# Relation attention, edge stage of a two-layer graph network: the mask goes into PSUM by matmuls, one maximum for all heads, the one-hot is transposed on TensorE

## The reference

```python
key_e = k_rel[edge_type, edge_src]
val_e = v_rel[edge_type, edge_src]
att = (q[edge_dst] * key_e).sum(-1) * rel_pri[edge_type] / jnp.sqrt(jnp.float32(dk))
seg = edge_dst * r + edge_type
amax = jax.ops.segment_max(att, seg, num_segments=S)
ex = jnp.exp(att - amax[seg])
denom = jax.ops.segment_sum(ex, seg, num_segments=S)
w = ex / denom[seg]
hsum = jax.ops.segment_sum(w[:, :, None] * val_e, seg, num_segments=S)
```

## Time and profile before

| what | us |
|---|---|
| median of three runs | 4749.34 |
| the three runs | 4734.86, 4749.34, 4750.56 |
| profiled execution, its span | 4737.6 |
| busy: PE, DVE, POOL, ACT | 4031.9, 4120.2, 3352.1, 2900.4 |
| HBM | 200 GB/s over the span |

### The profile page before, as it was taken

The page is one execution under the profiler, slowest core; times in us unless marked ns, Lnnn a source line. Parts: engine busy times, 40 slices in busy tenths (PEclk is TensorE's granted clock), DMA queues, the critical chain, the costliest instruction groups (busy, mean ns, idle before and its releaser), DMA issues. The chain is left out here.

```text
span 4737.6 us, 112614 instructions
## 1 busy us (share of the span) xinstructions
PE 4031.9 (85%) x23408; PEld 3334.4 (70%) x23408; DVE 4120.2 (87%) x13250; ACT 2900.4 (61%) x8405; POOL 3352.1 (71%) x3818
## 2 busy tenths in 40 slices
PE   0778888888888878999799898999999898968887
PEld 0357777777777767899677777777777677757776
DVE  6779999999999995555599999999999999968887
ACT  0765555555555543333488888888888888862222
POOL 0568888888888861111488888888888888857776
PEclk9989999999999998999888888888888888879899
DMA  2568777777777775666577777777777777776664
GB/s 75 179 206 250 229 228 228 228 228 227 228 229 228 228 190 174 202 200 197 168 207 206 204 206 204 206 204 205 205 204 206 204 204 204 205 158 189 176 170 133
DMA packets 647755, 950.12 MB, mean 201 GB/s; under 512 B 215768, under 2 KB 490760, under 8 KB 647287
## 3 DMA queue, kind: packets, MB, share of 16 engines
q0 software_dynamic: 153600, 510.70, 38.4%
q1 hardware_dynamic: 494043, 438.22, 32.1%
HBM read 777.56 MB, written 171.03 MB: 200 GB/s over the span
## 5 line engine op out<-in xcount | busy, mean ns | idle before, releaser
L1385 POOL DMA_INDIRECT kv1c<-kv_table,rec x936 | 916.8, 980 | 305.5 <-issue 175.2
L741 POOL DMA_INDIRECT kv<-kv_table,rec x864 | 921.3, 1066 | 247.3 <-issue 241.8
L1439 ACT ACTIVATE wv<-kv1c,wv 128x64 f32<-128x64 f32 x3744 | 927.7, 334 | 2.1
L1517 DVE CUSTOM_DVE_ANT_0 masked_scores<-score_p,mask 126x384 f32<-126x384 f32 x1248 | 679.5, 545 | 11.4 <-issue 5.8
L1615 PE MATMUL sum_p<-wv,hot 128*126 128x260 f32 x1872 | 626.3, 482 | 2.3 <-ACT wv L1439 2.3
L908 PE MATMUL sum_p<-msg,hot 128*126 128x256 f32 x1728 | 433.6, 394 | 192.2 <-DVE msg L864 192.2
L1577 PE MATMUL qe_p<-qrel,hotT 126*128 126x256 f32 x1872 | 546.9, 436 | 21.0 <-ACT hotT L1417 14.2
L1374 POOL TENSOR_SCALAR hot<-iota,local 128x126 f32<-128x126 f32 x936 | 549.7, 600 | 0.3 <-issue 0.2
L908 PEld LDWEIGHTS sum_p<-msg,hot 128*126 128x126 f32 x1728 | 309.4, 189 | 280.5 <-DVE msg L864 213.2
L1577 PEld LDWEIGHTS qe_p<-qrel,hotT 126*128 126x128 f32 x1872 | 428.8, 229 | 108.2 <-ACT hotT L1417 14.4
L1615 PEld LDWEIGHTS sum_p<-wv,hot 128*126 128x126 f32 x1872 | 398.4, 228 | 89.8 <-ACT wv L1439 2.7
(11 more groups left out here) (222 smaller groups left out, 10254.0 us busy)
## 6 DMA issues: line engine op xcount, KB each, us to landing
key<-segment_keys SPq DMA_DIRECT2D x312, 189.0 KB
q_blk<-q_table SPq DMA_DIRECT2D x216, 192.5 KB
acc_table<-acc SPq DMA_DIRECT2D x312, 128.0 KB
qrel<-q_by_relation SPq DMA_DIRECT2D x312, 126.0 KB
acc_in<-acc_table SPq DMA_DIRECT2D x50, 767.8 KB
q_by_relation<-qrel SPq DMA_DIRECT2D x50, 756.0 KB
feat<-in_edge_feat_t SPq DMA_DIRECT2D x216, 128.0 KB
agg_table<-total SPq DMA_DIRECT2D x216, 126.0 KB
```

What stands on the lines that cost most here:

```text
L741: pool.indirect_dma_start(kv[k][:, t, :], None, c["kv0_d"], bass.IndirectOffsetOnAxis(ap=rec[k][:, t, 0:1].bitcast(I32), axis=0)).then_inc ...
L1385: pool.indirect_dma_start(kv[k][:, t, :], None, c["kv1_d"], bass.IndirectOffsetOnAxis(ap=rec[k][:, t, 0:1].bitcast(I32), axis=0)).then_inc ...
L1439: ins = act.activation(wv[k][:, t, h, 0:DK], kv[s][:, t, D + h * DK:D + (h + 1) * DK], ACT.Copy, scale=wv[k][:, t, h, DK:DK + 1])
L1517: dve.tensor_tensor_reduce(junk[k][:, h, :], score_p[:, h, :], mask[it.slot(4)][:], 1.0, -BIG, ALU.add, ALU.max, top[s][:, h:h + 1]).then_ ...
```

## The change

In `edges_1`:

- The one-hot `hot` (edges by segments) is made by DVE in one instruction over all three tiles, at lag 0 (before: three on POOL at lag 1, behind `locate` on DVE). `locate` and the load of `key` go.
- ACT makes `cold` = 1 - hot in bf16 (lag 0); PE transposes it in three tiles (`turn_cold`, lag 1), and ACT makes the transposed one-hot in bf16 as 1 - cold, read from PSUM. `distances` and `masks` go.
- The mask gets into the scores' PSUM by three matmuls of 512 columns, cold times -2^100 on the diagonal, ahead of the twelve of `spread`, which now accumulate onto it.
- One `tensor_reduce` over 126x1536 takes the maxima of all four heads.
- `cap` goes; the split of the scores into bf16 parts moves from DVE to POOL (four small operations, between the gathers).
- The one-hot is bf16, so the queries come as three bf16 parts (nine matmuls of 256 columns in place of three f32) and the peak is split into three bf16 parts by four small operations on DVE (nine matmuls of 4 columns).
- ACT's scalings of values are split into three runs with other functions between.

In `nodes_1` the three bf16 parts of the queries are made: three copies on ACT, three subtractions on DVE, one more copy on ACT (126x1536) and one subtraction on POOL (126x1536). Each group's store grows from 756 to 1134 KB, each chunk's load of `qrel` from 126 to 189 KB.

The core of the diff:

```diff
@@ nodes_1
-                    for pair in range(1, PAIRS):
-                        ins = act.copy(qrel[k][:, 2 * pair:2 * pair + 2, :], rel_p[pair][:])
+                    for pair in range(PAIRS):
+                        act.copy(qrel[k][:, 2 * pair:2 * pair + 2, 0, :], rel_p[pair][:]).then_inc(rel_first, 1)
+                def rel_second_part(it):
+                    act.copy(qrel[k][:, :, 1, :], qrel_rest[k][:]).then_inc(rel_second, 1)
+                def rel_last_part(it):
+                    pool.tensor_tensor(qrel[k][:, :, 2, :], qrel_rest[k][:], qrel[k][:, :, 1, :],
+                                       ALU.subtract).then_inc(rel_last, 1)
+                def rel_left_over(it):
+                    for pair in range(PAIRS):
+                        dve.wait_ge(rel_first, it.count(0, PAIRS, pair + 1 - PAIRS))
+                        rels = slice(2 * pair, 2 * pair + 2)
+                        ins = dve.tensor_tensor(qrel_rest[k][:, rels, :], rel_p[pair][:], qrel[k][:, rels, 0, :],
+                                                ALU.subtract)
@@ relate (PE)
-                    wait(pe, rel_act, it, 1)
-                    wait(pe, rel_dve, it, 1)
+                    wait(pe, rel_left, it, 1)
@@ edges_1, POOL
-                run_chunks(pool, steps, ((5, fade_acc), (1, one_hot), (0, gather)))
+                run_chunks(pool, steps, ((0, gather((0,))), (2, lead_part(0)), (2, rest_part(0)), (2, lead_part(1)),
+                                         (2, rest_part(1)), (0, gather((1,))), (5, fade_acc), (0, gather((2,)))))
@@ ACT
+                def colds(it):
+                    wait(act, hot_ready, it)
+                    wait(act, spread_ready, it, 4)
+                    act.activation(cold[it.slot(4)][:], hot[it.slot(U)][:], ACT.Identity, bias=c["one"][:],
+                                   scale=-1.0).then_inc(cold_ready, 1)
                 def transposed_hot(it):
-                    wait(act, dist_ready, it)
+                    wait(act, coldT_turned, it)
-                run_chunks(act, steps, ((1, transposed_hot), (2, masks), (0, distances), (4, weights), (2, partsT_out)))
+                run_chunks(act, steps, ((4, weights), (0, colds), (4, values(0)), (1, transposed_hot), (4, values(1)),
+                                        (2, partsT_out), (4, values(2))))
@@ DVE
+                def one_hot(it):
+                    dve.scalar_tensor_tensor(
+                        hot[s][:], c["iota"][:].rearrange("p (o n) -> p o n", o=1).to_broadcast([P, T1, SEG]),
+                        par[s][:, 0:1], rec[s][:, :, 2:3].to_broadcast([P, T1, SEG]),
+                        ALU.add, ALU.is_equal).then_inc(hot_ready, 1)
-                        dve.tensor_tensor_reduce(junk[k][:, h, :], score_p[:, h, :], mask[it.slot(4)][:], 1.0, -BIG,
-                                                 ALU.add, ALU.max, top[s][:, h:h + 1]).then_inc(top_ready, 1)
+                    dve.tensor_reduce(top[s][:], score_p[:].rearrange("s t h e -> s h t e"),
+                                      mybir.AxisListType.XY, ALU.max).then_inc(top_ready, 1)
-                run_chunks(dve, steps, ((2, q_times_k), (4, below_peak), (2, scores), (4, cap), (0, locate),
-                                        (3, maxima(0)), (2, lead_part(0)), (3, maxima(1)), (2, rest_part(0)),
-                                        (3, maxima(2)), (2, lead_part(1)), (3, maxima(3)), (2, rest_part(1)),
-                                        (3, old_peak), (5, add_acc), (3, new_peak), (3, peak_drop)))
+                run_chunks(dve, steps, ((2, q_times_k), (4, below_peak), (2, scores), (3, old_peak), (0, one_hot),
+                                        (3, maxima), (5, add_acc), (3, new_peak), (3, peak_drop), (3, peak_part(0)),
+                                        (3, peak_part(1)), (3, peak_part(2)), (3, peak_part(3))))
@@ PE
+                def turn_cold(it):
+                    wait(pe, cold_ready, it)
+                    wait(pe, hotT_ready, it, 1)
+                    for t in range(T1):
+                        ins = pe.transpose(coldT_p[:, t * P:(t + 1) * P], cold[it.slot(4)][:, t, :], identity[:])
+                    ins.then_inc(coldT_turned, 1)
                 def q_of_edges(it):
-                        ins = pe.matmul(qe_p[:, t, :], hotT[k][:, t * P:(t + 1) * P], qrel[s][:], start=True, stop=True)
+                        for j in range(PARTS):
+                            ins = pe.matmul(qe_p[:, t, :], hotT[k][:, t * P:(t + 1) * P],
+                                            qrel[s][:, j * D:(j + 1) * D], start=j == 0, stop=j == PARTS - 1)
                 def spread(it):
+                    wait(pe, cold_ready, it)
+                    wait(pe, top_ready, it, 1)
+                    for t in range(T1):
+                        pe.matmul(score_p[:, t], cold[it.slot(4)][:, t, :],
+                                  mask_diag[:].rearrange("p (o e) -> p o e", o=1).to_broadcast([P, HEADS, P]),
+                                  start=True, stop=False)
                 def peaks_of_edges(it):
-                    wait(pe, peak_ready, it)
+                    wait(pe, peak_split, it, per=4)
+                            ins = pe.matmul(peak_p[:, t, :], hotT[k][:, t * P:(t + 1) * P],
+                                            peak_parts[it.slot(2)][:, j, :], start=j == 0, stop=j == PARTS - 1)
-                run_chunks(pe, steps, ((5, sum_values), (1, q_of_edges), (2, turn_parts), (3, peaks_of_edges),
-                                       (2, spread)))
+                run_chunks(pe, steps, ((5, sum_values), (1, turn_cold), (1, q_of_edges), (2, turn_parts),
+                                       (3, peaks_of_edges), (2, spread)))
```

`lead_part` and `rest_part`, written as before but for the engine, are on POOL now:

```diff
+                def lead_part(j):
+                        if j == 0:
+                            hold(pool, held, score_ready, it.count())
+                            wait(pool, partsT_turned, it, 2)
+                            pool.sem_inc(held, 1)
+                        else:
+                            hold(pool, held, split_ready, it.count(1, 4, 2 * j))
+                        pool.tensor_copy(parts[k][:, :, j, :], src[:]).then_inc(split_ready, 1)
```

More of the change, by code:

```diff
@@ L954, in nodes_1 @@
         qT_rest = [sb(f"qT_rest{k}", [P, HALF, GROUP], F32R) for k in range(2)]
-        qrel = [sb(f"qrel{k}", [GROUP, RELS, D]) for k in range(2)]
+        qrel = [sb(f"qrel{k}", [GROUP, RELS, PARTS, D], BF16) for k in range(2)]
+        qrel_rest = [sb(f"qrel_rest{k}", [GROUP, RELS, D]) for k in range(2)]
         agg_p = ps("agg_out_p", [P, 2, D])
@@ L1254, in edges_1 @@
     w0 = c["w0"]
+    Q1_ROW = PARTS * D
     with ExitStack() as ctx:
@@ L1282, in edges_1 @@
         peak = [sb(f"peak{k}", [SEG, HEADS]) for k in range(U)]
+        peak_rest = [sb(f"peak_rest{k}", [SEG, HEADS]) for k in range(2)]
+        peak_parts = [sb(f"peak_parts{k}", [SEG, PARTS, HEADS], BF16) for k in range(2)]
         drop = [sb(f"drop{k}", [SEG, HEADS]) for k in range(U)]
@@ L1367, in _ @@
                 steps = chunk_steps(pool, c["steps1"])
-                def one_hot(it):
-                    hold(pool, held, local_ready, it.count())
-                    wait(pool, summed, it, U)
-                    pool.sem_inc(held, 1)
-                    for t in range(T1):
-                        ins = pool.tensor_scalar(hot[it.slot(U)][:, t, :], c["iota"][:],
-                                                 local[it.slot(2)][:, t:t + 1], None, ALU.is_equal)
-                    ins.then_inc(hot_ready, 1)
@@ L1434, in weights, with values, f @@
                     act.activation(fade[s][:], drop[s][:], ACT.Exp).then_inc(fade_ready, 1)
-                    wait(act, weight_ready, it)
-                    wait_slot(act, gathered, it, T1)
-                    for t in range(T1):
+                def values(t):
+                    def f(it):
+                        k, s = it.slot(2), it.slot(U)
+                        if t == 0:
+                            wait(act, weight_ready, it)
+                            wait_slot(act, gathered, it, T1)
                         for h in range(HEADS):
@@ L1530, in new_peak @@
                     wait(dve, old_ready, it)
-                    wait(dve, top_ready, it, per=HEADS)
-                    wait(dve, of_edge_ready, it, U)
+                    wait(dve, top_ready, it)
+                    wait(dve, peak_split, it, U, per=4)
                     dve.scalar_tensor_tensor(peak[s][:], top[s][:], FLOOR, old[s][:], ALU.max,
@@ L1601, in peaks_of_edges @@
                     k = it.slot(4)
-                    wait(pe, peak_ready, it)
+                    wait(pe, peak_split, it, per=4)
                     wait(pe, diff_ready, it, 1)
                     for t in range(T1):
-                        ins = pe.matmul(peak_p[:, t, :], hotT[k][:, t * P:(t + 1) * P], peak[it.slot(U)][:],
-                                        start=True, stop=True)
+                        for j in range(PARTS):
```

(2 more changed lines are left out.)

237 lines of the change are left out of this document (110 added, 127 removed).

## The result

The changed kernel takes 5195.53 us (median of four, 5193.26 to 5210.93), against 4745.14 of the kernel before (four runs): ratio 1.0961, interval 1.094 to 1.0981. It is slower, as forecast, but by 450 us and not by 226.

What follows compares the result with a forecast made beforehand. POOL was taken to set the `edges_1` period of 6.10 us, other engines just behind. Period 6.8, +0.7 over 312 chunks, gives +218, `nodes_1` +8: 4749 + 226 = 4975 us, range 4700 to 5220.

Steps and rivals of the forecast that it cites:

- The loop from DVE over POOL to DVE: In `edges_1`, scores to POOL's parts, gather, fade_acc and back to add_acc: 3.55 plus 3.16, 6.71 us a chunk.
- Two loops that meet cost a little more than either: In `edges_1`, DVE-POOL and PE loops of 6.7 meet in add_acc and peaks_of_edges: period 6.8 us.
- PE's loop of 6.7: In `edges_1`, PE's work of 5.03 times 1.17 for low clock, plus 0.8 waiting for ACT's transposed one-hot.
- The parts on POOL: Four small score-splitting operations in `edges_1`, 0.3 us each, 1.2 a chunk (0.4 to 2.8 at the ends).
- DVE: DVE by itself in `edges_1`: 5.9 us a chunk, maximum 1.75, one-hot 0.6, no wait before the maximum.
- Loads: In `edges_1`, `key` goes and `qrel` grows by 63 KB: fewer bytes, one DMA issue less, costed at nothing.
- `nodes_1`: Stage with PE full: +8 us (0 to 60) from a longer last chain; DMA from 0.63 to about 0.78.
- POOL sets the period before: In `edges_1` of the kernel before, POOL is busy without gaps and sets the period, 6.09 us between first gathers.
- clock falls further: Rival: PE's mean clock in the edge stage falls to 0.75, loop 7.5 us, 5190 us; chance 0.15.
- small operations are dear: Rival: POOL's parts take 0.5 us each, 2.0 in all, loop 7.5, 5190 us; chance 0.12.
- the band of the forecast itself: Whole kernel: period 6.5 to 7.1 us in `edges_1`, 4882 to 5069 us; chance 0.53.

Runs made afterwards that it cites:

- The one run that freed POOL: Kernel before, with the one-hot as one DVE instruction in place of locate, POOL left with gathers and fade_acc only: 4985 us, ratio 1.0165.
- the kernel of 4658 us: Changed kernel with fade_acc first on POOL, turn_cold first on PE, transposed_hot right behind weights on ACT, and the peak kept in bf16: 4658 us, ratio 0.963.

## Why the prediction was right in sign and short in size

*The loop from DVE over POOL to DVE* (forecast 6.71): right in kind, shown by moving fade_acc both ways and by taking the splits out. Its size is 7.21. DVE's side was 3.55 and is 3.48. POOL's side was 3.16 and is 3.73, and this is the term mis-sized: the handovers, taken at 0.1 each, are 0.27 and 0.20; the first part, a cast, takes 0.363 and not 0.2, so the four take 1.33 for 1.2; the gap ahead of the gather is 0.30 for 0.16, the gather 0.98 for 0.95. Of the 0.57 too little, 0.27 are the handovers and 0.14 the gap.

*"Two loops that meet cost a little more than either"* (+0.1): failed. Between the loop's 7.21 and the mean of 7.62 lie 0.41, a wait of DVE for PE in about six of ten steps: for a sum at the low rate at acc, or for the queries before the product, three times in four behind such a sum. With the peak in bf16 the clock was 0.96 and 0.22 were left between loop and mean; with the mask twice it was 0.95 and 0.33 were left. The clock is thus part of the lateness, not all of it.

*PE's loop of 6.7*: at full rate, start to start, the queries take 1.09 for 0.93, the mask 0.77 for 0.65, the peaks 0.24 for 0.62, and the errors cancel by luck; its wait for the transposed one-hot is 265.1 / 288 = 0.92 for 0.8. It was not the bound: with that wait made shorter the kernel gained 30 us and less. The forecast took the mask matmuls as 0.65 a chunk on PE's path. They take that time, but leaving them out made the kernel 181 us slower by the clock, which the working had only as a factor that stays.

*The parts on POOL*: 0.36, 0.21, 0.19, 0.21, within 0.4 to 2.8 in all. The rule of the Trainium skill (GPSIMD Engine Reference, 4.1 Engine selection), about twice as slow as VectorE with two inputs, is not met at 12 elements: the two subtractions take 0.212 and 0.213 against 0.179 and 0.161 on DVE in the kernel before, 1.2 and 1.3 times. The page gives it for two inputs alone, and the prediction took it for the two casts as well.

*DVE*: the maximum takes 1.752 for 1.75, the one-hot 0.605 for 0.6. The forecast had no wait before the maximum; there are 98, 81.6 us in all, under the longer way over POOL. *Loads*: no cost, as forecast. *`nodes_1`*: +11 for +8, within the spread of chips; the DMA share rose to 0.71 and not 0.78 (its own working, 0.63 x 233 / 194, gives 0.76).

*POOL sets the period before*: it fits the first trace (a third of the steps 6.08 to 6.17, the rest from 5.2 to 7.4), but is not shown. The one run that freed POOL was slower, on a chip where the kernel before has gaps on POOL anyway. There the waits name DMA landings; whether they stood just behind POOL on the first chip is open.

*What no term had*: 24 us less in the last stage, whose code is the same. The kernel before has the clock at 0.88 and 0.91 there, the changed one 0.87 and 0.96. It was 471 to 484 us in every variant of the changed kernel but the two with the peak in bf16, which had 509 and 500, and 502 in the kernel before on another chip: it goes with the kernel and not with the chip. The cause is open.

The rival "clock falls further" had it at 0.75; it was 0.85, as before the change within 0.02, and acted as lateness added to another loop. The rival "small operations are dear" had the parts at 2.0; they took 1.33. Both were priced at 5190 us, and that the result is 5195 is luck: neither happened as described. The result lies outside the band of the forecast itself, 4882 to 5069, and in the range of 4700 to 5220 only near its upper end.

## What to carry to other kernels

When work moves to another engine, its place in that engine's list counts more than its length: an operation that another engine awaits stood behind four others and a gather, and setting it first took 0.9 us off a step of 7.6 without changing any work (a higher clock is part of it). Write the loop through both lists, add what the trace shows for a handover (here 0.27 us from DVE to POOL and 0.20 back), and check each awaited operation for what stands ahead of it. Here a second loop of nearly the same length was not hidden behind the first: its lateness came on top, 0.2 to 0.5 us a step. And a step whose tail feeds the next step's head gains from taking operations out of that tail (here four splits of 4 elements, worth a microsecond a chunk), while taking 1.9 us from POOL in the kernel before gained nothing on the chip where it was tried.

## What the runs showed of the hardware that was not expected

- Work on PE can pay for itself. Per chunk none, three and six mask matmuls of 512 columns gave mean granted clocks of 0.56, 0.83 to 0.85 and 0.95 in the stage, and periods of 8.33, 7.62 to 7.73 and 7.54 us. Without them 190 of 191 sums ran at the low rate. That a late PE makes the others late and so holds its own clock down fits this, but is argued. The last of these runs was on another chip than the first two.
- The same program can differ between chips by 3% (the kernel before, 4745 to 4892 us) and another, on two of them, by 0.5% (the changed one, 5195 and 5221). The waits of the slow runs name DMA landings; that these are the cause was not tested.
- An operation of 12 elements on POOL takes 0.19 to 0.21 us, a cast that follows a wait 0.36, and POOL starts 0.27 us after the DVE operation it waits for; DVE starts 0.20 after POOL's.
- POOL's `faded` and DVE's one-hot slow each other where they run at the same time: 0.63 us becomes up to 1.03, and 0.606 becomes 0.80 on average (the kernel of 4658 us).
